# Query rows in other partitions, key tables built by matmul, mask and maxima moved

## The reference

```python
q = (x @ Wq + bq); k = (y @ Wk + bk); v = (y @ Wv + bv)        # x is layernorm(x), y the context
att = scale * einsum('bthd,bThd->bhtT', q, k)
att = softmax(att * mask - 1e10 * (1.0 - mask))
x = x + einsum('bhtT,bThd->bthd', att, v) @ Wo + bo
h = relu(ln(x) @ w1[0] + b1[0]);  t = ln(x);  z = t + h @ w2[0] + b2[0]
out = x + layernorm(z) * gamma + beta                          # only expert 0 has weight 1
```

## Time and profile before

| | |
|---|---|
| median of 3 runs | 226.63 us (225.81 to 226.74) |
| the profiled execution | 226.6 us, of which its span 224.8 |
| TensorE busy | 198.1 us, 88% of the span, 1264 matmuls |
| VectorE, ScalarE, GpSimd busy | 148.7, 119.8, 80.8 us (66%, 53%, 36%) |
| queue q1, which carries the loads and stores of the kernel | 22.71 MB, 40.6% of 16 engines |
| chain that ended last | 65% TensorE, 18% DMA, 7% SP |

### The profile page before, as it was taken

The page is one execution under the profiler, slowest core; times in us unless marked ns, Lnnn a source line. Parts: engine busy times, 40 slices in busy tenths (PEclk is TensorE's granted clock), DMA queues, the critical chain, the costliest instruction groups (busy, mean ns, idle before and its releaser), DMA issues.

```text
span 224.8 us, 3534 instructions
## 1 busy us (share of the span) xinstructions
PE 198.1 (88%) x1264; PEld 153.4 (68%) x1264; DVE 148.7 (66%) x345; ACT 119.8 (53%) x216; POOL 80.8 (36%) x87
## 2 busy tenths in 40 slices
PE   0399979869968699798999999999999999999991
PEld 0376565437535557475879696667998899988990
DVE  0999999753936957454487219249664397895774
ACT  3298525826757085757725648986024960159200
POOL 4367952710000100598230104932245453371121
PEclk9999999967999999999999999999999999999999
DMA  6994498790999953995002230202000011010012
GB/s 216 382 358 141 152 242 187 140 260 0 208 211 230 211 130 73 156 175 110 5 1 74 71 70 4 73 0 96 0 0 3 0 48 47 3 47 0 3 70 70
DMA packets 14267, 23.99 MB, mean 107 GB/s; under 512 B 1716, under 2 KB 5300, under 8 KB 14250
## 3 DMA queue, kind: packets, MB, share of 16 engines
q1 hardware_dynamic: 13274, 22.71, 40.6%
q10 hardware_dynamic: 976, 1.06, 1.6%
HBM read 16.56 MB, written 6.55 MB: 103 GB/s over the span
## 4 chain that ended last, share of the span: by engine, by line
PE 65%; DMA 18%; SPq 7%; ACT 3%; issue 3%; DVE 2%; ACTq 0%; POOLq 0%; POOL 0%
DMA Sq<-nmx 7%; PE W L765 7%; PE W L768 6%; PE W L766 6%; PE acc L701 5%; PE W L751 5%; PE W L752 5%; PE W L753 5%; PE T L689 5%; DMA wk<-in_L_xattn_Wk_dram 3%; DMA wo<-in_L_xattn_Wo_dram 3%; DMA Sq<-qD 3%; PE M L668 2%; PE W L710 2%; DMA Mq<-qD 2%
## 5 line engine op out<-in xcount | busy, mean ns | idle before, releaser
L865 ACT ACTIVATE PT<-T 77x512 f32<-77x512 f32 x64 | 36.0, 591 | 21.8 <-PE T L689 20.2
L1005 DVE TENSOR_REDUCE mx<-M 128x6 f32<-128x462 f32 (+1 forms) x48 | 26.7, 579 | 19.9 <-PE M L668 19.7
L765 PE MATMUL W<-w2h,hh 128*128 128x256 f32 x128 | 36.6, 286 | 0.4 <-DVE aTl L1023 0.4
L768 PE MATMUL W<-w2h,hl 128*128 128x256 f32 x128 | 36.1, 282 | 0.0
L766 PE MATMUL W<-w2l,hh 128*128 128x256 f32 x128 | 36.1, 282 | 0.0
L689 PE MATMUL T<-Sq,KS 128*77 128x512 f32 x64 | 25.6, 431 | 7.7 <-DMA Sq<-nmx 5.5
L1180 POOL TENSOR_TENSOR hl<-hr,hh 128x512 fp32r<-128x512 f32 x12 | 16.1, 1338 | 43.6 <-ACT hh L911 43.6
L907 ACT ACTIVATE hr<-W,cst 128x512 f32<-128x512 f32 x32 | 22.0, 687 | 16.6 <-PE W L753 15.5
L751 PE MATMUL W<-x2h,w1h 128*128 128x512 f32 x64 | 25.8, 403 | 0.0
L765 PEld LDWEIGHTS W<-w2h,hh 128*128 128x128 f32 x128 | 24.1, 189 | 1.7 <-issue 1.5
L752 PE MATMUL W<-x2l,w1h 128*128 128x512 f32 x64 | 25.2, 394 | 0.0
(11 more groups left out here) (122 smaller groups left out, 407.9 us busy)
## 6 DMA issues: line engine op xcount, KB each, us to landing
Sq<-qD SPq DMA_DIRECT2D x16, 256.0 KB
xin<-in_x_dram SPq DMA_DIRECT2D x4, 512.0 KB, 7.5
qD<-qh SPq DMA_DIRECT2D x8, 256.0 KB, 3.7
qD<-ql SPq DMA_DIRECT2D x8, 256.0 KB, 3.6
Sq<-qD SPq DMA_DIRECT2D x16, 128.0 KB
out_dram<-xn SPq DMA_DIRECT2D x6, 256.0 KB, 2.0
Mq<-qD SPq DMA_DIRECT2D x6, 192.0 KB, 4.8
w1raw<-in_L_ffn_w_dram SPq DMA_DIRECT2D x2, 512.0 KB, 11.3
```

The lines of the kernel that those rows point to most:

```text
L765: e.matmul(y, hh[:, f, q:q + 128], w2h[:, f * E:(f + 1) * E], start=(f == 0), stop=False)
L768: i = e.matmul(y, hl[:, f, q:q + 128], w2h[:, f * E:(f + 1) * E], start=False, stop=(f == 7))
L865: e.activation(PT[:, m % 6, :], T[m % 2][0:TK, :], ACT.Exp).then_inc(exped, 1)
L1005: e.tensor_reduce(heads, M[(nth[step] - 1) % 2][:, 0:w * KP].rearrange("p (g h t) -> p g h t", g=1 if s < 2 else 2, t=KP)[:, :, :, 0:TK], ...
```

## The change

The query rows move to partitions 32 to 79 (Q0 = 32, Q1 = 80), in Sq in the order (feature, r) with r = high, low, high again. qD gets a third row for it, the store of the high part writes it twice, and the two loads of a quad become one. KM and KS are built whole by TensorE: each of the 12 key groups starts with a matmul of the identity (bf16) against a table eyer, the selection tables have 128 columns, and ScalarE and VectorE copy 128 partitions; eyem and ksid go. The mask of half 1 is copied from mT1 into Mq and Sq by GpSimd (maskm in six steps, masks in eight) and mD goes; three mask slots of half 0 go from VectorE to GpSimd (MSLOT_POOL). The maxima lie as (head, token block) in fp32r; one matmul against the negated identity identn transposes and negates eight heads of them into 32 rows, ScalarE copies 32 by 128, and quadm spreads 16 rows into partition 125. ScalarE scales chunks 1 to 3, with a shift that GpSimd works out. x of chunk 0 is loaded in two halves, by SP and by ScalarE's queue. All TIMES are new.

```diff
-Q0 = 64
-Q1 = 112
+Q0 = 32
+Q1 = 80
+SLOTS = (0, 1, 4, 2, 3, 5)
+FREED = (0, 1, 4, 5, 2, 3)
+MSLOT_POOL = 3
...
-        qD = [dram(f"qD{c}", (H, D, 2, 512)) for c in range(NC)]
+        qD = [dram(f"qD{c}", (H, D, 3, 512)) for c in range(NC)]
...
-            e.dma_start(xin[:, 0:4, :], x_v[:, row0(0)]).then_inc(ld_x[0], 16)
+            e.dma_start(xin[:, 0:2, :], x_v[:, row0(0), 0:2]).then_inc(ld_x0[0], 16)
...
-                elif kind == "maskm":
-                    i, = a
-                    n, first = ((4, 0), (2, 4))[i]
-                    fresh.wait_ge(m_out, 16)
-                    fresh.wait_ge(scored, nth["smax", 1, 3, 1 + i])
-                    for p, q in ((0, Q0), (Q1, MR)):
-                        e.dma_start(Mqf[p:q, first:first + n, :], mD[p:q, :].unsqueeze(1).to_broadcast([q - p, n, 512])
-                                    ).then_inc(ms_new[i], 16)
...
-                    e.dma_start(qD[c][8 * g:8 * g + 8, :, 0, :].rearrange("h d n -> (h d) n"),
-                                qh[:, 2 * (c % 2) + g, :].bitcast(F32)).then_inc(qh_out[2 * (c % 2) + g], 16)
+                    e.dma_start(qD[c][8 * g:8 * g + 8, :, 0:3:2, :].rearrange("h d r n -> (h d) r n"),
+                                qh[:, 2 * (c % 2) + g, :].bitcast(F32).unsqueeze(1).to_broadcast([P, 2, 512])
+                                ).then_inc(qh_out[2 * (c % 2) + g], 16)
...
+                        if c == 2:
+                            fresh.wait_ge(ms_new, 3 * g + 3)
...
+                    if u in (2 * NC, 2 * NC + 1):
+                        fresh.wait_ge(sq_new, 4 * (u - 2 * NC) + 4)
                     heads = qD[c][4 * k:4 * k + 4]
-                    e.dma_start(Sqf[Q0:Q0 + 32, s:s + 4, :], heads.rearrange("h d r n -> (d r) h n")).then_inc(sq_ld[u % 2], 16)
-                    e.dma_start(Sqf[Q0 + 32:Q1, s:s + 4, :],
-                                heads[:, :, 0, :].rearrange("h d n -> d h n")).then_inc(sq_ld[u % 2], 16)
+                    e.dma_start(Sqf[Q0:Q1, s:s + 4, :], heads.rearrange("h d r n -> (d r) h n")).then_inc(sq_ld[u % 2], 16)
...
+                    e.matmul(t[:, 0:2 * KP * len(heads)], identb[:, :], eyer[:, 0:2 * len(heads), :],
+                             start=True, stop=False)
...
-                    for n in range(4):
-                        i = e.transpose(t[0:r, n * 128:(n + 1) * 128], mx[:, c % 2, n, r * g:r * g + r], ident)
-                    i.then_inc(mx_turned, 1)
+                    e.matmul(t[0:32, 0:P], mx[:, c % 2, 8 * g:8 * g + 8, :].rearrange("p h n -> p (h n)"), identn[:, :],
+                             start=True, stop=True).then_inc(mx_turned, 1)
...
+                elif kind == "scale":
+                    c, = a
+                    fresh.wait_ge(x_shift, c)
...
+                    for n in range(4):
+                        i = e.activation(xn[:, c % 2, n, :], xin[:, 4 * c + n, :], ACT.Identity,
+                                         bias=x_nb[:, c, n:n + 1], scale=x_rs[:, c, n:n + 1])
+                    i.then_inc(x_normed_act, 1)
...
+                elif kind == "maskm":
+                    i, = a
+                    fresh.wait_ge(mT_made, 2)
+                    fresh.wait_ge(scored, nth["smax", 1, 3, (0, 2, 1)[i // 2]])
+                    e.tensor_copy(Mq[:, FREED[i], :], mT1[:, :].bitcast(F32)).then_inc(ms_new, 1)
+                elif kind == "masks":
+                    s, = a
+                    fresh.wait_ge(mT_made, 2)
+                    fresh.wait_ge(st_made, nth["st", 1, 8 + s])
+                    e.tensor_copy(Sq[:, s, :], mT1[:, :].bitcast(F32)).then_inc(sq_new, 1)
```

More of the change, by code:

```diff
@@ L139, in members @@
 def members(kind):
-    if kind in ("consts", "eyem", "sel", "flags", "crow", "bqr", "bk4", "mask", "splitwo", "statics"):
+    if kind in ("consts", "eyer", "sel", "flags", "crow", "bqr", "bk4", "mask", "splitwo"):
         return [[(kind,)]]
@@ L146, in members @@
         return [[(kind, to, g, j) for to in ("KM", "KS") for g in range(2) for j in range(3)]]
-    if kind in ("late", "ksid", "mslot", "sslot", "maskm", "masks"):
-        return [[(kind, i) for i in range({"late": 2, "ksid": 4, "mslot": 6, "sslot": 8, "maskm": 2, "masks": 2}[kind])]]
+    if kind in ("late", "mslot", "sslot", "maskm", "masks"):
+        return [[(kind, i) for i in range({"late": 4, "mslot": 6, "sslot": 8, "maskm": 6, "masks": 8}[kind])]]
     if kind == "split":
@@ L153, in members @@
     if kind == "mxt":
-        return [[(kind, c, g) for g in range(turns(c))] for c in range(NC)]
+        return [[(kind, c, g) for g in range(2)] for c in range(NC)]
     if kind in ("qproj", "qlow", "qload", "attn"):
@@ L168, in members @@
     return [[(kind, c)] for c in range(NC)]
[L171 to L178, removed]
 def pool_takes(step):
@@ L206, in has_part @@
     if step[0] == "mslot":
-        return (step[1] < 3) == (engine == "DVE")
+        return (step[1] < MSLOT_POOL) == (engine == "POOL")
+    if step[0] == "scale":
+        return (step[1] > 0) == (engine == "ACT")
     if step[0] == "low":
@@ L212, in has_part @@
     return True
-KINDS = ("consts", "eyem", "sel", "flags", "crow", "bqr", "bk4", "kproj", "mask", "mT", "values", "ksid", "mslot", "sslot",
-         "keys", "split", "splitwo", "statics", "late", "maskm", "masks", "norm", "scale", "turn", "xbias", "qproj", "qlow",
+KINDS = ("consts", "eyer", "sel", "flags", "crow", "bqr", "bk4", "kproj", "mask", "mT", "values", "mslot", "sslot",
+         "keys", "split", "splitwo", "late", "maskm", "masks", "norm", "scale", "turn", "xbias", "qproj", "qlow",
          "qload", "smax", "mxt", "quadq", "quadm", "st", "pv", "weigh", "attn", "proj", "scale2", "turn2", "bias2", "ffn1",
@@ L290, in build @@
         ql = sb("ql", [P, 2, 512], F32R)
-        mx = sb("mx", [P, 2, 4, H])
-        nmx = sb("nmx", [H, 2, 512], F32R)
-        PT = sb("PT", [TK, 6, 512])
+        mx = sb("mx", [P, 2, H, 4], F32R)
+        identn = sb("identn", [P, P], F32R)
+        mT1 = sb("mT1", [P, 512], F32R)
+        with ExitStack() as over:
+            sel_m, sel_h, sel_l = (over.enter_context(nc.sbuf_tensor(name, [P, 8, P], F32R))
+                                   for name in ("sel_m", "sel_h", "sel_l"))
+        PT = sb("PT", [P, 6, 512])
+        nmx = PT[96:P, 0, 0:256].bitcast(F32R).rearrange("p (g t) -> p g t", g=2)
         pvq = sb("pvq", [P, 2, 512])
@@ L330, in build @@
             wo = early("wo", [P, 2, E])
-            ctxT = early("ctxT", [P, 2, 2, TK])
+            ctxT = early("ctxT", [P, 2, 2, KP])
             mrow = early("mrow", [P, 8, TK])
             crow = early("crow", [P, 8, P], BF16)
-            mT = early("mT", [P, 1024], F32R)
+            mT0 = early("mT0", [P, 512], F32R)
             xn = early("xn", [P, 2, 4, E])
@@ L346, in build @@
         K3 = [T[0], T[1], acc]
-        ld_x = [sem(f"ld_x{c}") for c in range(NC)]
+        mT = [mT0, mT1]
+        ld_x0, ld_x = [sem("ld_x0a"), sem("ld_x0b")], [None] + [sem(f"ld_x{c}") for c in range(1, NC)]
         ld_c, ld_ctx, ld_wk, ld_m = sem("ld_c"), sem("ld_ctx"), sem("ld_wk"), sem("ld_m")
@@ L473, in loaded, with normed @@
             return 48 + 32 * c
+        def normed(c):
+            return (x_normed, 1) if c == 0 else (x_normed_act, c)
         def quad(c, k):
@@ L607, in tensor_program @@
                     fresh.wait_ge(mT_made, half(c) + 1)
-                    e.matmul(t[:, :], bqr[:, g, :], mT[:, 512 * half(c):512 * half(c) + 512],
-                             start=False, stop=True).then_inc(q_made, 1)
+                    e.matmul(t[:, :], bqr[:, g, :], mT[half(c)][:, :], start=False, stop=True).then_inc(q_made, 1)
                 elif kind == "kproj":
@@ L615, in tensor_program @@
                     for k in range(2):
-                        i = e.matmul(t[:, 0:2 * TK], wk[:, k, g * P:(g + 1) * P],
+                        i = e.matmul(t[:, 0:2 * KP], wk[:, k, g * P:(g + 1) * P],
                                      ctxT[:, k, :, :].rearrange("p b t -> p (b t)"), start=(k == 0), stop=(k == 1))
@@ L629, in tensor_program @@
                     fresh.wait_ge(*((k_high, g + 1) if to == "KM" else (k_split, g + 1)))
-                    for i, h in enumerate(range(3 * j, min(3 * j + 3, 8))):
-                        o = t[0:48, 2 * TK * i:2 * TK * (i + 1)]
-                        high = kh[:, g, :, :].rearrange("p b t -> p (b t)")
+                    heads = range(3 * j, min(3 * j + 3, 8))
+                    fresh.wait_ge(identb_made, 1)
+                    fresh.wait_ge(eyer_made, 1)
+                    e.matmul(t[:, 0:2 * KP * len(heads)], identb[:, :], eyer[:, 0:2 * len(heads), :],
+                             start=True, stop=False)
+                    high = kh[:, g, :, :].rearrange("p b t -> p (b t)")
+                    for i, h in enumerate(heads):
+                        last = i == len(heads) - 1
+                        o = t[:, 2 * KP * i:2 * KP * (i + 1)]
                         if to == "KM":
```

(69 more changed lines are left out.)

112 lines of the change are left out of this document (56 added, 56 removed), and 179 rows, old and new, of the table TIMES.

## The result

The changed kernel takes 213.3 us (median of 4 runs, 212.21 to 214.62) against 226.22 of the kernel before in the same runs: a ratio of 0.943, 95% interval 0.937 to 0.949, or 12.9 us less. Its profiled execution took 214.62 us with a span of 212.8, 12.0 less than before. Forecast were 8.8 us less and 217.8 us.

The account below looks back on a forecast made before the run. TensorE bounds the kernel, with 12.7 us idle, mostly on DMA landings of score operands, and 3.4 us of low clock. +0.2 + 0.5 - 1.5 - 1.3 - 1.7 - 4.4 - 1.6 + 1.0 = -8.8: 217.8 us, range 211.5 to 223.5.

Parts of the forecast that it names:

- the likeliest case: Whole kernel: the summed forecast of 217.8 us, own range 213.5 to 221, chance 0.55.
- TensorE's work: Key groups +3.1 us (selection matmuls 0.7, bounds 0 and 2.4), transposes of maxima -2.9: net +0.2 us.
- Start: First matmul's wait for wk, behind half of the first x chunk on ACT's queue: +0.5 us (0 to +1.4).
- VectorE: Relieved of scaling chunks 1 to 3 and three mask copies; TensorE's waits on it go: -1.5 us (0 to -2.5).
- The query rows: Quad loads into partitions 32 to 79: wider spread lifts the DMA rate from 215 to 320 GB/s (bounds 215 and 384).
- the three terms: Cuts in TensorE's DMA waits: early (before 46.7 us) -1.3, middle (56.2 to 84) -4.4, late (90 to 102) -1.6 us.
- The clock: TensorE's low clock in 45 to 56.2 us loses 3.4 us; half comes back: -1.7 us (0 to -3.4).
- The mask on GpSimd: Fourteen copies of about 0.68 us form new links that SP's loads wait behind: +1.0 us (-1 to +3).
- The rival in which all waits go: TensorE runs through from 9.5 us with about 195 us of work: -14.8, 211.8 us; chance 0.15.
- The slower rival: DMA rate stays at 215 GB/s, doubled stores cost 4.2 us between 24 and 50: +5.2, 231.8 us; chance 0.07.
- the signs named in advance: DMA over 300 GB/s, middle share under 0.8, idle some 5 us, clock over 0.85, last matmul near 211, scores about 36.
- the signs of being wrong: TensorE idle before L689 and L668 behind DMA, clock low for over 8 us, or SP long behind GpSimd's copies.

Follow-up runs that it names:

- the last variant: Changed kernel with the old order, the mask of half 1 by DMA and query rows in 64 to 111: 229.9 us, ratio 1.025 to the kernel before.

## Why the prediction was right, and where its sizes were off

The forecast, 217.8 us, had the direction and the mechanism; the time lies 4.5 us below it, just under the likeliest case's own range (from 213.5) and inside the whole one.

- **TensorE's work**, +0.2. It came to about +0.3: 195.0 us busy against 194.7. Within it the selection matmuls now follow at 0.11 us (L634 at 24.16, L635 at 24.27), not near the 0.07 of the earlier trace rows but at the pace of the other bound, so they cost 1.9 us, not 0.7. The identity matmuls add about 0.17, not 0.22, and a maxima transpose holds TensorE for 0.06 (45.54 to 45.60). These misses go against each other and largely cancel.

```profile
24.16 0.28 PE L634 MATMUL T<-kh,sel_h 128*128 128x156 f32 x1
24.27 0.28 PE L635 MATMUL T<-kl,sel_l 128*128 128x156 f32 x1
...
45.54 0.22 PE L672 MATMUL W<-identn,mx 128*32 128x128 f32 x1
45.60 0.41 PE L682 MATMUL T<-Sq,KS 128*77 128x512 f32 x1
```

- **Start**, +0.5, was 0: TensorE idles 7.7 + 1.3 = 9.0 us, as before, though wk lands a microsecond later, since the mask transposes run in that microsecond. The first scores came at 37.8.
- **VectorE**, -1.5: its waits are gone. With the scaling alone undone the kernel loses 1.4 us, so the sum's term stands as far as the runs can tell. Its basis does not: the 8.0 us of scaling were priced at 670 ns each, and put back they cost VectorE about half of that.
- **The query rows.** 320 GB/s per full share was taken; 322 is measured in 24 to 50.6 and 282 in 56.2 to 78.2, and undoing the range costs 13 us of DMA time. This step carried the forecast and held, in part by luck: the forecast gave the whole rise from 215 to the range, and in the early stage half of it came without (274 in partitions 64 to 111), while in the middle, where it is the range alone, the rate stayed short of 320. The early and late waits were cut too little: 10.6 us on DMA became 2.1, a cut of 8.5 where the three terms gave 1.3 + 4.4 + 1.6 = 7.3. The early one, halved in the forecast, went whole.
- **The clock**, -1.7: this is the term that was mis-sized most. Between the first key matmul and the last matmul no stall over 1.8 us is left, the clock stays at 1.00, and all of the 3.4 us came back. In the runs whose stalls came back (64 to 111, mask by DMA) it fell again and cost 5.1 us each time. The length of a stall alone does not decide it: the kernel before kept 1.00 after stalls of 2.2 us, and the run with a semaphore for the maxima fell to 0.92 in 56 to 78 us, behind one of 1.75.
- **The mask on GpSimd**, +1.0. The copies take 0.61 us each and held up nothing on VectorE: a reduction of maxima that ran beside one, at 54.17, took 0.63 us, the mean of its form (634 ns, 632 before). The prediction had given the rule of the Trainium skill (SBUF — State Buffer, Who interferes with whom) without its condition: the page lets GpSimd block only VectorE instructions in certain fast modes or with two inputs in SBUF, and excepts reductions on this chip. What ran beside these copies read PSUM for the most part, so the case shows no harm there; the scalings, which read and write SBUF, are the ones that were slower beside GpSimd (3.69 us for four against 1.38). A new wait of 1.7 us did come, but from ScalarE's semaphore, which the forecast did not name. What the prediction missed is that the copies make room for an order: I priced the new links at +1.0 and the DMA time that the copies free at 4.3 us in the middle, and in the new order they are worth 14 us.

The sum of what happened, by span: +0.3 work, -8.5 DMA waits, -1.5 VectorE, -3.4 clock, +1.7 new wait, and 0.6 less of small gaps, -12.0. The rival in which all waits go (211.8 us) was the nearer one. The slower rival did not come, since the rate rose. The run that has its condition, the slow range with all else as changed, took 223.7 us, level with the kernel before beside it, where the rival had 5.2 us more and 231.8: its price was 5 to 8 us too high, and which of its terms was is not shown. The 229.9 us of the last variant are near its figure by luck, as that run lacks the copies and the new order, which the rival kept.

Of the signs named in advance, DMA over 300 GB/s at full share held early but not in the middle, the share under 0.8 held (0.55), TensorE's idle time in 24 to 110 came to 3.6 (some 5 named), the last matmul to 207.8 (211 named), the first scores to 37.8 (36 named). Of the signs of being wrong, idle time before the scores with DMA as its end is still there, but it is 1.9 us; the clock did not fall, and SP did not stand long behind GpSimd's copies (4.4 us in all for those into Sq).

## What to carry to other kernels

Divide GB/s by the DMA share, stage by stage: where full engines move half of what they move elsewhere, look at which partitions the loads go to before cutting bytes or issues. The worth of a part depends on the order around it: the mask copies brought 2 us in one order and 14 in another, so parts measured alone don't add up, and a part that takes a link out of a chain should be priced together with the order it allows. A stall is dearer than its length when the clock falls behind it (in two variants some 5 us on top of 4 and 8 of waiting), and a false wait is worth nothing when the next true one ends at the same time.

## What was not expected of the hardware

Two ranges of 48 partitions that share 32 of them, 16 to 63 and 32 to 79, differ by 7 us of kernel time (220.9 and 213.5 us) with the same bytes and packets. And the 156-column matmuls with a full stationary operand follow each other at 0.11 us, nearly the 0.12 of the 256-column ones, while with 48 stationary columns they follow at 0.07. In these rows the pace goes with the columns of the stationary operand and hardly with those that stream; that the stationary operand sets it is a reading of them, which no run tests.
